# Token-major heads of a state-space layer: 32x32 block transposes on VectorE and 16 SBUF-to-SBUF transfers per unit in place of TensorE's transposes

## What is computed

```python
proj = einsum('bsd,ed->bse', layernorm(x), in_proj_w)       # gate | hs, B, C | dt
hBC  = silu(causal_conv4(hBC) + conv_b)                     # hs: 8192 channels
xch  = hs * dt                                              # per head
Y_diag = einsum('bzlhn,bzshn,bhzls,bzshp->bzlhp', C, B, L, xch)      # inside a chunk
states = einsum('bzlhn,bhzl,bzlhp->bzhpn', B, decay_states, xch)     # carried over chunks
Y_off  = einsum('bzlhn,bzhpn,bhzl->bzlhp', C, prev_states, exp(A_cum))
y   = (Y_diag + Y_off + hs * D) * silu(gate)
x   = x + einsum('bsi,oi->bso', rmsnorm_by_group(y) * norm_w, out_proj_w)
x   = x + layernorm(x) @ W.T + b + low_rank_experts(layernorm(x))
```

## Time and profile before

| | |
|---|---|
| median of 3 runs | 1605.16 us (1605.1 to 1605.87) |
| span of the profiled execution | 1605.0 us |
| TensorE busy | 1583.5 us, 99% |
| VectorE busy | 1264.2 us, 79% |
| ScalarE busy | 1163.1 us, 72% |
| GpSimd busy | 700.7 us, 44% |
| DMA | 162.37 MB, mean 101 GB/s, queue of SP 30.8% of 16 engines |
| mean granted TensorE clock | 0.998 |

### The profile page before, as it was taken

How to read it: one execution, slowest core, us unless ns; L and a number is a source line. 1 busy time by engine, 2 the same in 40 slices (tenths; PEclk the granted TensorE clock), 3 DMA queues, 4 the chain that set the end, 5 groups by cost and what they waited for, 6 DMA issues and landing times.

```text
span 1605.0 us, 26714 instructions
## 1 busy us (share of the span) xinstructions
PE 1583.5 (99%) x9576; PEld 1346.1 (84%) x9576; DVE 1264.2 (79%) x1984; ACT 1163.1 (72%) x2027; POOL 700.7 (44%) x535
## 2 busy tenths in 40 slices
PE   7899999999999999999999999999999999999998
PEld 5688888888888888888888888888888888888887
DVE  6687777877778777887778877787877878788787
ACT  5887667776777677777687766777677767777753
POOL 2155444453444454354453544445344445435550
PEclk9999999999999999999999999999999999999999
DMA  4542322332323233332232232233232323223211
GB/s 151 192 145 86 122 89 83 112 112 73 112 97 114 73 109 95 98 106 92 99 108 97 86 122 89 83 112 112 73 112 99 113 73 109 99 92 112 93 44 53
DMA packets 86916, 162.37 MB, mean 101 GB/s; under 512 B 23040, under 2 KB 39424, under 8 KB 86528
## 3 DMA queue, kind: packets, MB, share of 16 engines
q1 hardware_dynamic: 86784, 160.66, 30.8%
HBM read 154.84 MB, written 5.77 MB: 100 GB/s over the span
## 4 chain that ended last, share of the span: by engine, by line
PE 97%; DVE 1%; ACT 1%; issue 0%; DMA 0%; SPq 0%; DVEq 0%; ACTq 0%
PE g_bank L778 10%; PE g_bank L780 9%; PE g_bank L779 9%; PE d_bank L797 7%; PE x_bank L778 7%; PE x_bank L780 7%; PE x_bank L779 7%; PE head_bank L786 5%; PE head_bank L804 5%; PE x_bank L836 4%; PE x_bank L837 4%; PE x_bank L835 4%; PE d_bank L837 4%; PE d_bank L835 4%; PE d_bank L836 4%; PE head_bank L812 3%
## 5 line engine op out<-in xcount | busy, mean ns | idle before, releaser
L1448 POOL TENSOR_TENSOR w_low<-raw,w_high 128x512 fp32r<-128x512 f32 x139 | 179.8, 1294 | 553.5 <-ACT w_high L1011 553.5
L1199 DVE SCALAR_TENSOR_TENSOR hs<-x_bank,cols,hs 128x1022 f32<-128x1022 f32 x189 | 241.6, 1278 | 129.7 <-ACT hs L1033 127.5
L1021 ACT ACTIVATE scores<-scores,tables 128x128 f32<-128x128 f32 x1024 | 312.4, 391 | 0.0
L1462 POOL TENSOR_TENSOR y<-y,gate 128x512 f32<-128x512 f32 x128 | 185.4, 1467 | 198.8 <-DVE y L1268 198.8
L1033 ACT ACTIVATE hs<-x_bank,cols 128x1024 f32<-128x1024 f32 x63 | 75.9, 1204 | 269.9 <-PE x_bank L780 269.9
L778 PE MATMUL g_bank<-x_high,w_high 128*128 128x512 f32 x624 | 250.8, 402 | 0.0
L779 PE MATMUL g_bank<-x_low,w_high 128*128 128x512 f32 x624 | 243.2, 390 | 0.0
L780 PE MATMUL g_bank<-x_high,w_low 128*128 128x512 f32 x624 | 243.1, 390 | 0.0
L778 PE MATMUL x_bank<-x_high,w_high 128*128 128x512 f32 x504 | 196.3, 390 | 0.1
L780 PE MATMUL x_bank<-x_high,w_low 128*128 128x512 f32 x504 | 196.1, 389 | 0.0
L779 PE MATMUL x_bank<-x_low,w_high 128*128 128x512 f32 x504 | 196.1, 389 | 0.0
(11 more groups left out here) (211 smaller groups left out, 3433.3 us busy)
## 6 DMA issues: line engine op xcount, KB each, us to landing
scores<-sums_dram SPq DMA_DIRECT2D x128, 512.0 KB, 4.8
raw<-w_in SPq DMA_DIRECT2D x144, 256.0 KB, 2.9
grown_rows<-grown_dram SPq DMA_DIRECT2D x256, 96.0 KB, 2.8
out_raw<-w_out SPq DMA_DIRECT2D x64, 256.0 KB, 3.4
mixed<-x SPq DMA_DIRECT2D x8, 256.0 KB, 5.1
out<-mixed SPq DMA_DIRECT2D x8, 256.0 KB, 2.0
table_dram<-table SPq DMA_DIRECT2D x2, 768.0 KB, 5.3
tables<-table_dram SPq DMA_DIRECT2D x30, 48.0 KB, 2.7
```

Of the source, the lines that this page charges most:

```text
L1021: op = s.activation(at, at, ACT.Relu, bias=col[:, r, c:c + 1], scale=-1.0)
L1199: v.scalar_tensor_tensor(out=hs[:, q % 2, :, i:], in0=x_bank[:, :, 0:SEQ - i], scalar=cols[:, q, TAPS - 1 - i:TAPS - i], in1=hs[:, q % 2, ...
L1448: pool.tensor_tensor(w_low[:, slot], raw[:, slot], w_high[:, slot].bitcast(F32), ALU.subtract)\
L1462: pool.tensor_tensor(y[:, b], y[:, b], gate[:, q % 2, b], ALU.mult).then_inc(y_ready, 1)
```

## The change

TensorE's `turn_hs` is dropped but for unit 0 (`turn_first`). For every other unit VectorE's `turn_blocks(k)` transposes the 32x32 blocks of `hs` inside each quarter of 32 partitions and writes them over the `hs` buffer of the unit before, which is free after its `skip`. SP's `move_blocks(k)` then moves the blocks between the quarters: 4 x 4 transfers from SBUF to SBUF, each of 32 partitions and 256 elements (1 KB) a partition, into a new tile `quads`. `to_heads` reads `quads` in SBUF, one instruction for each head over both batches (it was one for each batch), and stands behind both `score`s of its iteration. `diagonal` and `decayed` wait for both of its halves. On VectorE the three taps stand together ahead of `carried_state`, and `squares_of` stands behind `y_low_part`. On ScalarE the second `differences` stands ahead of the gate's Silu and both `decays` (Exp) at the end of the iteration. On SP the first weight load of the next iteration is issued earlier (in most iterations ahead of `move_blocks`), and `load_grown` stands behind `move_blocks`. `bias_high` and `bias_low` share memory with `out_high` and `out_low`.

```diff
+            def move_blocks(k):
+                sp.wait_ge(blocks_turned, k)
+                sp.wait_ge(xdt_ready, PAIR * k)
+                blocks = blocks_of(k)
+                for m in range(QUADS):
+                    for a in range(QUADS):
+                        sp.dma_start(quads[m * QUAD:(m + 1) * QUAD, a].rearrange("p b c i -> p (b c i)"),
+                                     blocks[a * QUAD:(a + 1) * QUAD, m * SEQ // 2:(m + 1) * SEQ // 2])\
+                          .then_inc(moved[m], 16)
...
+                    then = splits_after(g, last, j, 2)[:1]
+                    for at in then if len(splits) < SPLIT else []:
+                        load_weight(*at)
                     if ahead:
+                        move_blocks(ahead[2])
                         for b in range(BATCH):
                             load_grown(ahead[2], b)
+                    for at in then if len(splits) == SPLIT else []:
+                        load_weight(*at)
...
             def states(k, b):
                 pe.wait_ge(xdecay_ready, BATCH * k + b + 1)
+                reached(pe, carry_scaled, BATCH * (k - 1) + b + 1)
...
-                pe.wait_ge(xdt_ready, BATCH * k + b + 1)
+                pe.wait_ge(xdt_ready, PAIR * (k + 1))
...
-                    if ahead:
-                        for b in range(BATCH):
-                            turn_hs(k + 1, (j + 1) % 2, b)
...
                     if ahead:
                         differences(k + 1, ahead[0], ahead[1], 0)
-                        decays(k + 1, ahead[1], 0)
                         silu_hs(k + 1, (j + 1) % 2)
+                        differences(k + 1, ahead[0], ahead[1], 1)
...
                     if ahead:
-                        differences(k + 1, ahead[0], ahead[1], 1)
-                        decays(k + 1, ahead[1], 1)
+                        for b in range(BATCH):
+                            decays(k + 1, ahead[1], b)
...
+            def turn_blocks(k):
+                v.wait_ge(hs_ready, k + 1)
+                v.wait_ge(skip_added, k)
+                v.transpose(blocks_of(k).rearrange("p (m n i) -> p n m i", m=QUADS, i=QUAD),
+                            hs[:, k % 2].rearrange("p b (c m i) -> p (b c) m i", c=CHUNKS, i=QUAD))\
+                 .then_inc(blocks_turned, 1)
+
+            def to_heads(g, q, k):
+                for m in range(QUADS):
+                    v.wait_ge(moved[m], 16 * QUADS * k)
...
+                for r in range(PAIR):
+                    col = tables[:, :, q // HALF, DT, PAIR * (q % HALF) + r]
+                    v.tensor_tensor(xdt[:, :, :, r],
+                                    quads[:, r * PER_HEAD:(r + 1) * PER_HEAD].rearrange("p h b c i -> p (b c) h i"),
+                                    col.unsqueeze(3).to_broadcast([P, BATCH, CHUNKS, HEAD_DIM]), ALU.mult)\
+                     .then_inc(xdt_ready, 1)
...
-                    for b in range(BATCH):
-                        to_heads(g, j, k, b)
-                    if j == 1 and g > 0:
-                        squares_of(g)
...
                         score(g, j, k, 1)
+                    if k > 0:
+                        to_heads(g, j, k)
...
                     if j == 1 and g > 0:
+                        squares_of(g)
                         group_rstd(g)
...
                     if ahead:
-                        tap(1, *ahead)
+                        for i in range(1, TAPS):
+                            tap(i, *ahead)
                     for b in range(BATCH):
                         carried_state(*now, b)
                     if ahead:
-                        tap(2, *ahead)
-                        tap(3, *ahead)
                         skip(j, k)
+                        turn_blocks(k + 1)
```

More of the change, by code:

```diff
@@ L36 @@
 DMA_SCRATCH = 8192
+QUAD = 32
+QUADS = P // QUAD
+PER_HEAD = HEAD_DIM // QUAD
 def reached(eng, semaphore, value):
@@ L81, in emptied, with splits_after @@
     return CHUNKS * (k - 2) + c + 1
+def splits_after(g, last, j, by):
+    if j + by < UNITS:
+        return splits_of(g, last, j + by)
+    return [] if last else splits_of(g + 1, False, j + by - UNITS)
 def flushed(j):
@@ L620, in mixer @@
         ident_r = sb("ident_r", [P, P], F32R)
-        bias_high, bias_low = sb("bias_high", [P, HID], F32R), sb("bias_low", [P, HID], F32R)
+        quads = sb("quads", [P, QUADS, BATCH, CHUNKS, QUAD])
+        bias_high, bias_low = out_high[:, 0], out_low[:, 0]
         g_std, g_rstd, squares = sb("g_std", [P, TB]), sb("g_rstd", [P, TB]), sb("squares", [P, TB])
@@ L627, in mixer @@
         chunk_in = [[sem(f"chunk_in{b}_{h}") for h in range(2)] for b in range(BATCH)]
+        blocks_turned, moved = sem("blocks_turned"), [sem(f"moved{m}") for m in range(QUADS)]
         names = ("gate_ready", "hs_ready", "turned", "xdt_ready", "xdecay_ready", "relu_ready", "exp_ready",
@@ L716, in body @@
                     ahead, second = unit(g, last, j + 1), unit(g, last, j + 2)
[L717 to L720, removed]
+                    splits = splits_after(g, last, j, 1)
                     if k == 2:
                         first_dense(sp)
-                    for at in splits[:1]:
-                        load_weight(*at)
                     if ahead:
@@ L761, in _ @@
             load_weight(0, place(0, 2) + 1)
+            for at in splits_after(0, False, 0, 1)[:1]:
+                load_weight(*at)
             over_groups(sp, body)
@@ L806, in carry, with turn_first @@
                 mm.then_inc(carried, 1)
[L808 to L810 removed]
+            def turn_first(b):
+                pe.wait_ge(hs_ready, 1)
                 for c in range(CHUNKS):
[L812 removed]
+                    mm = pe.transpose(head_bank[b][:, c * P:(c + 1) * P], hs[:, 0, b, c * P:(c + 1) * P], ident[:])
                 mm.then_inc(turned, 1)
@@ L859, in product_of @@
                     pe.wait_ge(bias_low_ready, 1)
-                pe.matmul(to, ident_r[:], bias_high[:], start=True, stop=False)
-                pe.matmul(to, ident_r[:], bias_low[:], start=False, stop=False)
+                pe.matmul(to, ident_r[:], bias_high, start=True, stop=False)
+                pe.matmul(to, ident_r[:], bias_low, start=False, stop=False)
                 pe.wait_ge(xt_ready, tb + 1)
@@ L1269, in add_carry, with first_heads @@
                  .then_inc(y_sum, 1)
[L1271 to L1274, removed]
-                reached(v, diag_done, BATCH * (k - 1) + b + 1)
-                reached(v, xdecay_ready, BATCH * (k - 1) + b + 1)
-                col = table_of(DT, b, q).rearrange("p r c -> p c r")
+            def first_heads(b):
+                v.wait_ge(tables_in[b][0], 16)
+                v.wait_ge(turned, b + 1)
+                col = table_of(DT, b, 0).rearrange("p r c -> p c r")
                 v.tensor_tensor(xdt[:, b], head_bank[b].rearrange("p (c r d) -> p c r d", c=CHUNKS, r=PAIR),
@@ L1280, in to_heads @@
                  .then_inc(xdt_ready, 1)
+            def turn_blocks(k):
[5 more added lines that the diff above has]
+            def to_heads(g, q, k):
+                for m in range(QUADS):
+                    v.wait_ge(moved[m], 16 * QUADS * k)
+                v.wait_ge(diag_done, BATCH * k)
+                v.wait_ge(xdecay_ready, BATCH * k)
+                if q % HALF == 0:
+                    for b in range(BATCH):
+                        v.wait_ge(tables_in[b][q // HALF], 16 * (g + 1))
+                for r in range(PAIR):
[4 more added lines that the diff above has]
+                     .then_inc(xdt_ready, 1)
             def keep_bc(g, src):
@@ L1360, in body @@
                     prev, now, ahead = (unit(g, last, j + i) for i in range(-1, 2))
-                    for b in range(BATCH):
-                        to_heads(g, j, k, b)
-                    if j == 1 and g > 0:
-                        squares_of(g)
+                    if k == 0:
+                        for b in range(BATCH):
+                            first_heads(b)
                     if k > 2:
```

14 lines of the change are left out of this document (9 added, 5 removed).

## The result

The changed kernel takes **1787.93 us** (median of 4 runs, 1785.53 to 1791.1) against 1605.13 us (1605.02 to 1605.87): a ratio of 1.1138, with a 95% interval of 1.1122 to 1.1154. It is slower, as forecast, but by 183 us instead of 44, outside the range of 1560 to 1725. The profiled execution has a span of 1786.2 us.

What follows compares the result with a forecast made beforehand. The prediction took TensorE's ordered work as the bound. Dropping the transposes saves 7.2 us per group but stalls add 12.7, so some 5.5 more per group, 44 for eight: 1649 us, range 1560 to 1725.

Steps and rivals of the forecast that it cites:

- What bound the kernel, and what the transposes cost: TensorE's ordered work sets the time; its transposes cost 0.90 us in each of 63 units, 57 us.
- The signs named: Profile after: TensorE idle 2 to 4 us before `states` in j = 0, 2, 3, 4; VectorE awaiting transfers before `to_heads`.
- The chain's parts: From first tap on VectorE: turned blocks at 8.55 us, `quads` full at 18.9, `to_heads` done at 20.15, `states` at 22.3.
- the price of SP's issues: On SP's queue, each of 16 transfers takes 0.55 us to issue, with 0.38 and 0.63 as ends.
- the rival with this price: SP's issues priced as 64-partition rows or above: about 51 us more over five units of each group, 1700 us; chance 0.25.
- TensorE has more to do ... than the chain needs: In j = 4 to 6 TensorE's own work covers the new chain: 76.1 us for the three units.
- the floor of 1548: Whole kernel if everything replacing TensorE's transposes is hidden: 1605 - 57 = 1548 us.
- The turns between VectorE and GpSimd: Two-SBUF-input VectorE instructions and GpSimd's `decayed` alternate: `states` 2.15 us after `to_heads`, 0.8 more in j = 2 and 3.
- Costed at nothing: Other moves, such as `load_grown` behind the 16 issues and both Exp at the end of ScalarE's iteration: no cost.
- the sum on record: Eight unit lengths on TensorE added up: 195.9 us a group against 190.5, some 5.5 more.
- That it fits: Chain hidden and kernel faster: SP issues at 0.38 us give 1569 us, break-even about 0.46 us; chance 0.33.
- The slow transposes: VectorE's block transposes take 2.4 us, making chain and VectorE's loop 1.15 us longer: some 1695 us; chance 0.07.

Runs made afterwards that it cites:

- the best version: Changed kernel with blocks moved through DRAM, `to_heads` ahead of the B and C taps, transfers ahead of held weight loads, bias in `quads`: 1596.65 us.
- experiments 4: Changed kernel with only twelve or eight of the 16 transfers, the rest of `quads` constant: 1683.29 us and 1612.08 us.
- experiment 5: Changed kernel with the 16 transfers replaced by one store to DRAM and four loads of 32 partitions each: 1628.53 us.
- experiment 2: Changed kernel without transfers (`quads` constant), with `to_heads` of j = 5 and 6 ahead of the three taps of B and C: 1584.74 us.
- experiment 3: Changed kernel without transfers, `to_heads` ahead of the B and C taps in j = 5 and 6, norm and `y_low_part` ahead of `to_heads`: 1671.83 us.
- Experiment 8: Changed kernel with 12 to 18 dummy products on TensorE ahead of the wait of `states` in j = 0, 2, 3 and 4: 1778.93 us.
- experiment 10: The best version, 1596.65 us, and one run of it without the move of the bias into `quads`, 1600.08 us.

## Why the prediction was off

**What bound the kernel, and what the transposes cost: right.** TensorE was the path, and a unit without transposes and stalls takes the forecast time: 26.6 and 22.9 us in j = 5 and 6 of the best version, against 27.5 and 23.8.

**The signs named.** From the second group on TensorE stalls before `states` in j = 0, 2, 3 and 4, as forecast, but by 2.7 to 5.2 us instead of 2 to 4. VectorE waits there for the transfers before `to_heads`.

**The chain's parts.** The block transpose takes 1.25 us, as taken. To the turned blocks it is 8.9 us (8.55 predicted), from the start of the last issue to `to_heads` 2.1 (2.1), `to_heads` 1.2 (1.25).

**The step that failed first is the price of SP's issues.** I took the middle of 0.47 and 0.63, 0.55 us. It is 0.63, as in the row of 64 partitions, and the 16 take 10.0 to 11.2 us: in a third of the series one issue takes up to 1.7. Of the rival with this price, 1700 us, the mechanism holds: all that is above 1612 us comes with the transfers beyond the eighth, and all but 16 us of it goes when they are issued in less time (experiments 4 and 5). That the row of 64 partitions gave the right price says less than it seems. The loads of experiment 5 have 32 partitions and cost 0.43, and an issue of all 128 partitions costs 0.58 right behind a `grown_rows`:

```profile
979.54 2.51 SPq L705 DMA_DIRECT2D grown_rows<-grown_dram  x4
982.10 0.58 SPq L694 DMA_DIRECT2D out_raw<-w_out  x1
```

What sets the price is open.

**The second is a step that I did not take: where `to_heads` was moved to in j = 5 and 6.** I wrote that in j = 4 to 6 "TensorE has more to do ... than the chain needs". That looked at the transfers' chain and not at VectorE's order, in which three taps of 3.9 us now stand ahead of `to_heads`. Without transfers it costs 24 us (experiment 2). It is also 24 of the 61 us by which the kernel without transfers misses the floor of 1548; the other 37 are told in experiment 3.

**The third: what a stall does to the next instructions.** My unit lengths on TensorE keep `states` at its old 1.5 us and `diagonal` at 2.0. After stalls of 2.7 us and more the granted clock falls and they take up to 2.9 and 3.6 us. Experiment 8 puts this at some 10 us.

**The turns between VectorE and GpSimd: right in kind, wrong in part.** I took a pair of `decayed` near 2.9 us; it takes 2.61 behind `y_low_part` and 3.06 with `normed_out`, and the three `normed_out` 4.25 instead of 3.65. But the 0.8 us more before `states` in j = 2 and 3 is not there: `states` starts 3.24 us after `to_heads` in j = 1 to 4 alike, and the longer pair makes only its second half late. So j = 3 does not get the 0.8 us that I took off it. VectorE's loop in j = 2 was to be 25.0 us and is 27.1: of the 2.1, 1.2 are issues, 0.3 the way to the blocks, 0.5 the norms.

**Costed at nothing:** `load_grown` and the Exp, rightly by the profile: no wait for the rows is in it, and the waits for the Exp are 1.4 us in all. Not rightly the bias: the kernel's end, from the last `states` on, is 64.1 us after (1786.2 - 1722.1) and 58.2 before (1605.0 - 1546.8). Of these 6 us some 2 are the last unit's `states` and `diagonal` at the lower clock (2.9 us each, against 1.5 and 2.2), and some 4 the wait that experiment 10 removes.

**What it adds up to.** The miss is 139 us (1788 - 1649). In the mean of groups 1 to 6 a group is 16.5 us longer than the sum on record: 2.1 in j = 0, 1.4 in j = 1, 2.4 in j = 2, 3.1 in j = 3, 5.6 in j = 4 to 6 and 2.0 in j = 7. Eight times that and the 6 us of the end are 138. Of a group's 16.5, 6 are the issues (1.2 in each of five units, as the rival counted) and 5.6 are in j = 4 to 6, where the order on VectorE and the clock meet. The rest, some 5 us a group, I put down to the way to the blocks, the longer norms, the clock and the uneven issues; these were not run by themselves. Why an issue in some series takes a microsecond longer stays open.

**The other rivals.** That it fits (chance 0.33) was wrong by its condition: of the 1008 issues no two are less than 0.56 us apart. The slow transposes were wrong: 1.25 us. The rule of the Trainium skill's page "VectorE: DVE Perf Modes", section "Rules for kernel authors", to use TensorE for 128 x 128 transposes if PSUM will do, held for the change as made (1788 us against 1605). The best version, which is at 1597 with the transposes on VectorE, shows that it isn't the block transpose that loses but the 16 small transfers and the order around them.

## What to carry to other kernels

A queue's issues are a serial resource like an engine: count them on the path before counting bytes or landings. A small error in their price is multiplied by the issues and by the units: 0.08 us here came to some 50. Where a producer is moved within an engine's order, list what stands ahead of it in every kind of iteration, the rare ones too: without transfers a late place cost 24 us here. The same reordering may gain or lose, as it falls into a wait or makes one.

## What was not expected of the hardware

- An issue of 32 partitions x 1 KB from SBUF to SBUF costs SP 0.63 us in a series, as one of 64 partitions does; one of 32 partitions x 4 rows of 1 KB from DRAM costs 0.47, and the series of SBUF issues moves 512 KB in 10 us where one store of 512 KB is issued in 0.32.
- SP's and ScalarE's queues issue side by side without slowing each other (8 each in 5.1 and 5.4 us).
- In 30 of 31 stalls of 2.7 us or more, or right behind them, TensorE's granted clock fell to 1.2 GHz for a few us; with dummy products in the stalls it mostly stays at 2.4 GHz (0.985 against 0.955 over the span).
